# Two graph layers in one kernel: 9-row matmuls of the attention loop padded to 128 rows

## The reference, cut to what matters

```python
h = relu(layernorm(x))
def type_proj(W, b):                       # W [3, 128, 128], b [3, 128]
    all_t = einsum('ni,tio->tno', node_inp, W) + b[:, None, :]
    return all_t[node_type, rng]           # each node takes the matrix and bias of its own type
k, q, v = type_proj(Wk, bk), type_proj(Wq, bq), type_proj(Wv, bv)
...                                        # per edge: key and message by relation, attention by head
res = trans * a + node_inp * (1.0 - a)     # trans holds the bias ba of the node's type
normed = (res - mu) * rsqrt(var + 1e-05)
return normed * ln_g[node_type] + ln_b[node_type]
```

## Time and profile before

| | us |
|---|---|
| median of 3 runs | 2772.43 (2771.65 to 2778.87) |
| the profiled execution | 2774.48 |
| span of its trace (first to last instruction) | 2772.8 |
| attention loop in it, L986's first to L1086's last record | 366.8 to 1404.5 |
| edge phase and convolutions (first L1419 on) | 1480.4 to 2772.8 |

### The profile page before, as it was taken

The page is one execution under the profiler, slowest core; times in us unless marked ns, Lnnn a source line. Parts: engine busy times, 40 slices in busy tenths (PEclk is TensorE's granted clock), DMA queues, the critical chain, the costliest instruction groups (busy, mean ns, idle before and its releaser), DMA issues. The chain is left out here.

```text
span 2772.8 us, 48253 instructions
## 1 busy us (share of the span) xinstructions
PE 1846.7 (67%) x12706; PEld 1451.0 (52%) x12706; DVE 2019.8 (73%) x6947; ACT 1176.9 (42%) x3234; POOL 1676.0 (60%) x1763
## 2 busy tenths in 40 slices
PE   3640069999999999999935888883555533333333
PEld 0110059999999999999933555552444322222221
DVE  7999769999999999999967999994444433333333
ACT  0000047777777777777723666662222211111111
POOL 0005567777777777777613656564666567667666
PEclk9985579999999999999967999895555555555555
DMA  7007957777777767777613555553444422222221
GB/s 198 0 0 256 349 154 183 184 180 179 181 181 183 186 181 182 185 182 182 175 43 85 144 143 152 145 135 92 110 111 118 107 65 66 63 62 66 61 65 47
DMA packets 425001, 373.00 MB, mean 135 GB/s; under 512 B 47762, under 2 KB 379390, under 8 KB 421760
## 3 DMA queue, kind: packets, MB, share of 16 engines
q1 hardware_dynamic: 385584, 275.36, 36.9%
q0 software_dynamic: 31360, 64.76, 11.3%
q10 hardware_dynamic: 7806, 29.98, 2.7%
HBM read 226.63 MB, written 146.53 MB: 135 GB/s over the span
## 5 line engine op out<-in xcount | busy, mean ns | idle before, releaser
L1674 DVE TENSOR_TENSOR_SCAN conv_sT<-keep,conv_sT,conv_pT 128x128 f32<-128x128 bf16 x390 | 186.7, 479 | 488.4 <-DMA t<-conv_res 202.8
L1655 PE MATMUL conv_pm<-w,conv_sT 128*128 128x128 f32 x784 | 279.8, 460 | 378.1 <-DVE conv_res L1681 236.3
L792 POOL DMA_INDIRECT att_xsd<-xt,ends_i x392 | 390.2, 995 | 95.1 <-issue 94.9
L1655 PEld LDWEIGHTS conv_pm<-w,conv_sT 128*128 128x128 f32 x784 | 196.3, 310 | 471.8 <-issue 313.6
L973 PE MATMUL att_kvc<-att_hm,w_kv 128*128 128x128 f32 x2352 | 296.9, 276 | 0.0
L1086 DVE TENSOR_TENSOR att_kvm<-att_kvc,att_rel_in 128x1024 f32<-128x1024 f32 x196 | 240.1, 1225 | 63.5 <-PE att_kvc L986 62.3
L973 PEld LDWEIGHTS att_kvc<-att_hm,w_kv 128*128 128x128 f32 x2352 | 280.8, 193 | 0.0
L1634 ACT ACTIVATE conv_row<-conv_row,ats 128x128 f32<-128x128 f32 x196 | 78.7, 401 | 474.6 <-DMA conv_row<-t,idx 457.9
L1603 POOL DMA_INDIRECT out_dram<-conv_res,out_i x196 | 197.5, 1008 | 112.6 <-issue 99.9
L1649 PE MATMUL conv_pT<-ident,conv_row 128*128 128x128 f32 x392 | 168.0, 429 | 134.5 <-issue 109.0
L1597 POOL DMA_INDIRECT conv_row<-ta,idx x196 | 185.0, 944 | 105.1 <-issue 43.5
(11 more groups left out here) (240 smaller groups left out, 4817.7 us busy)
## 6 DMA issues: line engine op xcount, KB each, us to landing
att_mask_in_t<-type_row SPq DMA_DIRECT2D x196, 192.0 KB
xt<-xr ACTq DMA_DIRECT2D x23, 1224.0 KB
att_nxr<-xt SPq DMA_DIRECT2D x97, 262.0 KB
att_rel_in<-rel_row SPq DMA_DIRECT2D x196, 128.0 KB
out_dram<-att_not SPq DMA_DIRECT2D x97, 256.0 KB
ta<-att_nhs SPq DMA_DIRECT2D x97, 256.0 KB
xr<-in_x_dram SPq DMA_DIRECT2D x20, 1088.0 KB
xd_rows<-att_xsd SPq DMA_DIRECT2D x196, 65.5 KB
```

What stands on the lines that cost most here:

```text
L792: pool.indirect_dma_start(out=xsd[:, v, k, :], out_offset=None, in_=xt, in_offset=bass.IndirectOffsetOnAxis(ap=ends_i[:, n, k:k + 1], axis ...
L1655: nc.tensor.matmul(pm[:, k % 2, 0:D], sT[:, k % R], w[:], start=True, stop=True).then_inc(m_ready, 1)
L1674: dve.tensor_tensor_scan(sT[:, n % R], keep[:, n * P:(n + 1) * P], pT[:, n % 2, 0:P], before, ALU.mult, ALU.add).then_inc(s_ready, 1)
```

## The change

`bias9`, `typesT`, the five `noh` buffers and `tab9` get 128 partitions in place of 9. The rows past the ninth hold zeros: `tab9` is zeroed by a memset in the setup, the other seven by memsets of DVE at the loop's start, each of which counts up the new semaphore `blank`. SP and ACT wait for all seven before their first work in the loop. What writes into the buffers afterwards writes 9 partitions as before. The products L974, L976, L986 and L995 now take the whole buffers and so contract over 128 rows, of which 119 are zero; their results are the same. The edge phase still slices `tab9` to 9 rows.

```diff
-        tab9 = sb("tab9", [K9, CW + GW], BF16)
+        tab9 = sb("tab9", [P, CW + GW], BF16)
...
+                    dve.memset(tab9[:], 0.0).then_inc(vec, 1)
-                    n[0] = 2
+                    n[0] = 3
...
-            typesT = lb("typesT", [K9, 4, 2, P], BF16)
+            typesT = lb("typesT", [P, 4, 2, P], BF16)
...
-            bias9 = lb("bias9", [K9, 3, D], BF16)
+            bias9 = lb("bias9", [P, 3, D], BF16)
...
-            noh = [lb(f"noh{b}", [K9, NJ * P], BF16) for b in range(RO)]
+            noh = [lb(f"noh{b}", [P, NJ * P], BF16) for b in range(RO)]
...
                 def _(sp):
+                    sp.wait_ge(blank, RO + 2)
...
-                        sp.dma_start(noh[g % RO][:, 0:j * P], node_hot[:, n0:n0 + j * P]).then_inc(noh_in[g % RO], 16)
+                        sp.dma_start(noh[g % RO][0:K9, 0:j * P], node_hot[:, n0:n0 + j * P]).then_inc(noh_in[g % RO], 16)
...
                 def _(act):
+                    act.wait_ge(blank, RO + 2)
...
-                            nc.scalar.activation(typesT[:, k % 4], tT[:, 0:2], ACT.Copy).then_inc(types_out, 1)
+                            nc.scalar.activation(typesT[0:K9, k % 4], tT[:, 0:2], ACT.Copy).then_inc(types_out, 1)
...
+                    for tile in [typesT, bias9] + noh:
+                        dve.memset(tile[:], 0.0).then_inc(blank, 1)
                     dve.memset(nmv[0][:], 1.0).then_inc(nst_done, 1)
...
-                            nc.tensor.matmul(pc[g % 2][:, j], oh[g % 4][:, j * P:(j + 1) * P], tab9[:, 0:D], start=False, stop=False)
+                            nc.tensor.matmul(pc[g % 2][:, j], oh[g % 4][:, j * P:(j + 1) * P], tab9[0:K9, 0:D], start=False, stop=False)
```

More of the change, by code:

```diff
@@ L611, in _ @@
                     link(dve.tensor_scalar(tab_f[:, D:CW], sk9[:], -1.0, 1.0, ALU.mult, ALU.add))
-                    for f, r, p, o, part in ((bias_f, bias_r, bias_p, bias3, 0), (tab_f, tab_r, tab_p, tab9, 1)):
+                    for f, r, p, o, part in ((bias_f, bias_r, bias_p, bias3[:], 0), (tab_f, tab_r, tab_p, tab9[0:K9], 1)):
                         link(dve.tensor_copy(p[:, 0], f[:]))
@@ L622, in _ @@
                             if k == 0:
-                                link(dve.tensor_scalar(o[:], p[:, k], rowk[0:rows_n, 2:3], None, ALU.mult))
+                                link(dve.tensor_scalar(o, p[:, k], rowk[0:rows_n, 2:3], None, ALU.mult))
                             else:
-                                link(dve.scalar_tensor_tensor(o[:], p[:, k], rowk[0:rows_n, 2:3], o[:], ALU.mult, ALU.add))
+                                link(dve.scalar_tensor_tensor(o, p[:, k], rowk[0:rows_n, 2:3], o, ALU.mult, ALU.add))
                     dve.wait_ge(hists, ET)
@@ L738, in hgt_then_graphconv @@
             gb = lp("gb", [P, 2, GW], F32)
-            bias_in, made = ls("bias_in"), ls("made")
+            bias_in, made, blank = ls("bias_in"), ls("made"), ls("blank")
             got = [ls(f"got{u}") for u in range(RX)]
@@ L1446, in gains @@
                         for j in range(j0, j1):
-                            m = nc.tensor.matmul(pg[:, j - j0], oh[g % 4][:, j * P:(j + 1) * P], tab9[:, CW:CW + GW], start=True, stop=True)
+                            m = nc.tensor.matmul(pg[:, j - j0], oh[g % 4][:, j * P:(j + 1) * P], tab9[0:K9, CW:CW + GW], start=True, stop=True)
                         m.then_inc(pg_ready, 1)
```

## The result

| | before | changed |
|---|---|---|
| median of 9 runs | 2771.65 us (2763.51 to 2779.85) | 2755.28 us (2750.44 to 2761.46) |
| ratio | | 0.9938, 95% interval 0.9926 to 0.9949 |
| span of the trace | 2772.8 | 2752.2 |
| L1086 (now L1091), first to last start | 382.5 to 1403.3 | 385.2 to 1380.1 |

The kernel became faster by 0.62%, 16.4 us, where 36 us were forecast. In the two traces the loop's full part is 25.9 us shorter (994.9 against 1020.8), it begins 2.7 us later, and the rest behind it is 2.6 us longer: together the 20.6 us between the spans. That is 4.2 us more than between the medians, because the profiled execution of before lies 2.8 us over its median and that of the changed kernel 1.4 us under its own.

What follows compares the result with a forecast made beforehand. PE was taken to bound the loop, DVE 0.34 us a step behind. From the profiled 2774.5 us, less 190 x 0.20, plus 2.1, came 2738.6, or 2736.5 on the median's scale; range 2717 to 2778.

Steps and rivals of the forecast that it cites:

- The block's edges: PE's gaps into and out of the 9-row block: caused by row count, their removal takes 5.20 us to 4.95.
- The products: The block's seven bfloat16 products a step: reading 128 rows leaves their time and 0.055 us pitch unchanged.
- the rival that priced them at 0.11: Block's five distances on PE go to 0.11, +0.27 us a step; time near 2778 or 2826; chance 0.05.
- Around it: Outside the loop's steps: seven memsets delay SP's first DMA and first loads, +2.1 us; other phases unchanged.
- What DVE makes of it: Handover between PE (4.95 us) and DVE (4.92) in the loop decides the step; 5.04 us taken.
- fast end: Loop step at PE's own floor, 4.95 us; total 2719 us.
- slow end: Loop step set by the chain of late news through DVE: 10.2 us for two steps, 5.11 for one.
- the middle: Loop step of 5.04 us, from 5.24, over 190 steps; forecast 2736.5 us.
- the chain holds in full: Every second loop step stays 0.7 us late, DVE's L1097 holds L970: step 5.11 to 5.13, 2752 us; chance 0.25.
- The chain itself: In the loop, late L1086, next L1086, L1097, L970, L986, late again: 10.2 us for two steps.
- The signs: Profile checks: block-edge starts 0.11 apart, inner starts still 0.11, PE and DVE shares, first L832 at about 361.
- The third: Loop's middle: PE busy below 0.99, DVE about 0.97, DVE's waits for L986 from 42.6 us to below 20.

Runs made afterwards that it cites:

- e1: Changed kernel with only bias9 and typesT at 128 rows, noh and tab9 back at 9: ratio 1.0017 against the kernel before, fast chip.
- e2: Changed kernel with the padded buffers at 64 rows in place of 128: ratio 1.0010 against the kernel before, fast chip.
- e5: Changed kernel without DVE's addition of the second gain part (L1116): ratio 0.9880 against the kernel before, slow chip.
- e6: Changed kernel, PE's two waits for DVE behind L973, first loads ahead of bias DMAs, edge phase's one-hot buffers padded: 0.9864 against the kernel before, slow chip.
- e7: The changed kernel itself, unaltered, run again on the slow chip: ratio 0.9936 against the kernel before.
- e9: The changed kernel itself, unaltered, run on the fast chip: 2629.92 us against 2673.49 for the kernel before, ratio 0.9841.
- e4_nogather_after: Changed kernel without POOL's two gathers a step, SP loading same-sized rows instead: ratio 0.9828 against the kernel before, slow chip.
- e4_nogather_before: Kernel before without POOL's gathers in the loop, SP loading same-sized rows instead: ratio 1.0020 against the kernel before, fast chip.
- e3_waits_before: Kernel before with PE's waits for kvm_ready and res_done moved behind its three first products: ratio 0.9998 against it, fast chip.

## Why the prediction was right in sign and wrong in size

*The block's edges: right.* 0.096, 0.011, 0.09 and 0.056 us went, PE's own step is 4.95, and the reason chosen (rows, not type) is shown by e1 and e2.

*The products: right.* 128 rows of bfloat16 keep the 0.055; the rival that priced them at 0.11 is out.

*Around it: right.* The memsets took 0.48 + 0.22 + 1.37 us and SP's first DMA starts 2.27 us after POOL's first memset, where before they started together (358.86 and 358.85); 2.1 was forecast. DVE's first L1091 is 2.7 us later.

*What DVE makes of it: the step that failed.* The prediction had a fast end of 4.95 us, a slow end of 5.11 from the chain of late news, and took the middle, 5.04, with 190 x 0.20 = 38 us. Measured in that pair: 5.12, 190 x 0.12 = 23 us (25.9 between the starts of L1086 and L1091 in the two traces), which is the rival "the chain holds in full" with its 5.11 to 5.13 and 2752 us. The middle rested on the hope that the delay would fall away or be hidden when PE became faster and L976's end shifted against whatever holds the news. The opposite came: L979's end still falls inside one of POOL's gathers in every second step, so the delay stayed, and its mean rose from 0.84 to 0.96 us. "I can't name its cause from this trace" gave up too early: the POOL rows of the trace of before had it, with 66 of 67 late ends inside an L792. There was no ground for a value between the ends: each is a regime of its own, and in every trace here the loop stays in one. On the fast chip it is in the other, 4.98, and there the gain of 44 us is more than the forecast of 36. The forecast of 5.04 fits neither.

*The chain itself:* its shape was right as far as it went (L973 waits for L1102 in nearly every step), and 10.24 us for two steps were measured where 10.2 was worked out. That agreement is partly luck, as two terms were off and cancel: the part from the late L1091 to the next, for which a "usual" 5.3 was assumed that no row shows, measured 5.09, and the news from L989 to L1091 was 0.93 late where 0.7 stood in the sum. e5 and e6 show that it is not the only path. Shortening DVE's share or moving PE's waits on the slow chip brought 0.04 and 0.02 us a step beside 5.12 (0.06 and 0.04 beside e7's 5.14), not 0.16.

*The signs:* the starts at the block's edges and inside it came as named, and so did the shift of SP's first DMA, though at 360.17 and not 361, since the loop begins 1 us earlier in that trace. The third didn't come: PE's busy share stayed at 0.995 and didn't fall below 0.99 (matmul records overlap: of the 0.39 us hole in the starts above only 0.22 count as idle), DVE rose to 0.95 and not 0.97, and L1091's wait fell to 31.7 us and not below 20. The last two belong to the chain rival. The range of 2717 to 2778 holds the result because it spans both regimes and the case of no change; that the result lies in it says little.

**Open:** what in POOL's gathers holds PE's completions, and why on one chip only. One more difference stands in the traces. For the changed kernel between 600 and 1300 us the slow chip's trace holds 11,999 records of semaphore updates (e7), the fast chip's 19,729 (e9); without the gathers the slow chip's holds 20,359 (e4_nogather_after). So where PE's updates come late, records of others' are missing (of DVE's 136 updates by L1126 in e7's trace 11 are there). All runs were timed with their spans and clocks recorded, and whether the recording itself takes part in the delay was not tested. Whether the late news costs the convolutions time too (they gather as well, and they make up most of the 100 us between the two chips: from the first to the last start of L1649, L1654 now, 848 us on the slow chip in the trace of before, 751 on the fast one in e9) wasn't tried. Nor was e4_nogather_before obtained on the slow chip: that the kernel before loses little to the late news there rests on its step alone, 5.24 against the 5.20 of e3_waits_before on the fast chip, about 8 us of the loop.

## What to carry to other kernels

A matmul with few contraction rows among full ones costs at both edges of its block, about 0.25 us together here; padding the whole block with zero rows removes it at the price of a few memsets, while padding half of it removes nothing. Before booking a saving on a full engine, look at the engine that is even with it, and price each regime by itself; where two regimes are far apart, forecast one of them, not their mean. An engine that starts nearly a microsecond after the recorded end of what it waits for is a finding to follow up: look at what every other engine does at the late ends and at those on time, and compare the same pair of rows on another run or chip.

## What the runs showed of the hardware

- The switch between matmuls of 128 and of 9 or 64 rows costs 0.096 us going in (before, e2; in e1 between two bfloat16 products) and 0.09 plus 0.056 coming out (L1003 of before, L1006 of e2); 112 against 128 rows costs nothing (before, L1422 to L1432). In the edge phase the way out costs 0.09 and about 0.05: L1438's second record follows its first by 0.213 us in the trace of before, and by 0.165 (L1453) in e6, where all rows are 128. The pitch is 0.112, so another 0.05 there isn't the row count's.
- On chip 0, completions of PE that fall inside an indirect DMA instruction of POOL reach their waiters 0.8 to 1.0 us late in the mean (before, after, e7); outside of one (but for 2 of 70 in after's trace and 4 of 70 in e7's) it is 0.037 to 0.048 us, and without gathers (e4_nogather_after) 0.037. On chips 11 and 12 it is 0.037 us always. Late news of other engines was not seen: where their updates are recorded on chip 0, they stand at most 0.013 us after the end.
- The kernel before takes 2672 to 2673 us on chips 11 and 12 and 2775 us on chip 0.
